# A two-layer graph network on one core: VectorE's copies, the second norm and the convolution steps moved to other units of a round, and the moments of y moved into the first layer

## The reference, cut to what matters

```
h = relu(layernorm(x));  x = x + L0(h, adj)       # 8 Euler steps of a linear flow on the graph
h = relu(layernorm(x));  x = x + L1(h, adj)

L1: L_norm = 2 L / lam_max(L) - I                 # L is adj itself here; one matrix for all batches
    x1 = relu(layernorm((L_norm x) Wc + bc) g1 + be1) + x
    q, k, v = x1 Wq, x1 Wk, x1 Wv                 # 4 heads of 32
    o = softmax(where(adj > 0, q k^T / sqrt(32), -1e9)) v
    x2 = layernorm(x1 + o Wo + bo) g2 + be2
    out = layernorm(x2 + gelu(x2 W1 + b1) W2 + b2) g3 + be3
```

## Time and profile before

| | |
|---|---|
| median of three runs | 867.99 us |
| the profiled execution | 868.01 us |
| its span (first to last instruction) | 866.2 us |
| PE busy | 818.8 us (95%) |
| DVE busy | 646.5 us (75%) |
| ACT busy | 530.5 us (61%) |
| POOL busy | 310.4 us (36%) |
| mean granted clock | 0.988 |

### The profile page before, as it was taken

One profiled execution on the slowest core, in us unless ns is written; L12 is line 12 of the kernel. 1 busy time (PEld: TensorE's weight loads), 2 busy tenths in 40 slices (PEclk: granted clock), 3 DMA queues, 4 the chain that ended last, 5 costly groups with the idle time before them and its releaser, 6 DMA issues.

```text
span 866.2 us, 18914 instructions
## 1 busy us (share of the span) xinstructions
PE 818.8 (95%) x6609; PEld 690.4 (80%) x6609; DVE 646.5 (75%) x2146; ACT 530.5 (61%) x1223; POOL 310.4 (36%) x406
## 2 busy tenths in 40 slices
PE   6999999999999999998999999999999999999992
PEld 5778989898989888976777777777777777778982
DVE  5956464645477656536899999999999998987998
ACT  4434243434322422325988888898888888887884
POOL 2011121212122415300445545555554545432654
PEclk9999999999999999998999999999999999999997
DMA  6000010101010100312434455423344444322243
GB/s 133 1 13 13 13 37 13 37 14 37 13 37 13 37 25 26 101 46 76 119 94 108 133 136 135 134 94 96 96 124 135 135 136 133 103 49 63 82 139 97
DMA packets 57514, 65.59 MB, mean 76 GB/s; under 512 B 5574, under 2 KB 32844, under 8 KB 57420
## 3 DMA queue, kind: packets, MB, share of 16 engines
q1 hardware_dynamic: 57120, 64.25, 26.6%
q10 hardware_dynamic: 300, 0.13, 0.1%
HBM read 39.59 MB, written 24.77 MB: 74 GB/s over the span
## 4 chain that ended last, share of the span: by engine, by line
PE 21%; DVE 12%; issue 8%; POOL 8%; ACT 3%; DMA 1%; DVEq 0%; SPq 0%; POOLq 0%
PE bank L1896 6%; PE bank L1954 4%; PE bank L1916 4%; PE bank L1882 3%; DVE prob L2062 2%; PE bank L381 2%; POOL z_norm L353 2%; POOL z_gain L349 2%; POOL x_bo L1834 2%; DVE stats L1666 2%; ACT prob L2004 2%; POOL rstd_b L230 2%; PE bank L385 1%; DVE prob L1661 1%; DVE z L2101 1%
## 5 line engine op out<-in xcount | busy, mean ns | idle before, releaser
L2004 ACT ACTIVATE prob<-prob,low 128x512 f32<-128x512 f32 x256 | 183.7, 718 | 28.2 <-DVE low L2062 25.8
L2062 DVE CUSTOM_DVE_ANT_0 prob<-bank,mask 128x512 f32<-128x512 f32 x256 | 171.0, 682 | 8.5 <-PE bank L1882 6.3
L1896 PE MATMUL bank<-ident,prob 128*128 128x128 f32 x1024 | 158.3, 277 | 1.4 <-ACT probT L1987 1.0
L1896 PEld LDWEIGHTS bank<-ident,prob 128*128 128x128 f32 x1024 | 120.8, 141 | 42.1 <-issue 30.6
L1882 PE MATMUL bank<-k_stack,q_stack 96*128 96x512 f32 x256 | 124.1, 485 | 8.6 <-DVE low L2062 7.3
L1987 ACT ACTIVATE probT<-bank 128x512 f32<-128x512 f32 x176 | 103.1, 586 | 22.9 <-PE bank L1896 21.4
L880 PE MATMUL bank<-B_hi,halves 128*128 128x384 f32 x384 | 106.7, 341 | 3.0 <-DVE C L1276 1.6
L851 PE MATMUL bank<-halves,P3T_hi 128*128 128x256 f32 x512 | 93.9, 285 | 0.9 <-DVE halves L1292 0.5
L851 PEld LDWEIGHTS bank<-halves,P3T_hi 128*128 128x128 f32 x512 | 80.5, 191 | 4.4 <-DVE halves L1292 1.3
L880 PEld LDWEIGHTS bank<-B_hi,halves 128*128 128x128 f32 x384 | 70.6, 189 | 6.4 <-DVE halves L1263 2.7
L851 PE MATMUL bank<-halves,P3T_lo 128*128 128x256 f32 x256 | 72.4, 283 | 0.0
(11 more groups left out here) (277 smaller groups left out, 1919.4 us busy)
## 6 DMA issues: line engine op xcount, KB each, us to landing
k_stack<-bounce_q SPq DMA_DIRECT2D x48, 256.0 KB, 4.0
q_stack<-bounce_k SPq DMA_DIRECT2D x48, 256.0 KB, 5.5
bounce_q<-k_parts SPq DMA_DIRECT2D x32, 256.0 KB, 2.2
bounce_k<-q_parts SPq DMA_DIRECT2D x32, 256.0 KB, 3.8
x_in<-in_x_dram SPq DMA_DIRECT2D x16, 256.0 KB, 2.8
spread<-inverse_sums SPq DMA_DIRECT2D x64, 64.0 KB, 2.1
out_dram<-probT SPq DMA_DIRECT2D x16, 256.0 KB, 2.4
y_shifted<-y_staging SPq DMA_DIRECT2D x14, 256.0 KB, 2.1
```

The costliest lines, as they stand in the source:

```text
L1896: last = pe.transpose(psum[2 + u % 2][:, mt * P:(mt + 1) * P], prob[u % RING][:, mt * P:(mt + 1) * P], ident[:, :])
L2004: act.activation(prob[u % RING][:, :], prob[u % RING][:, :], ACT.Exp, bias=low[:, u % TURNED:u % TURNED + 1], scale=-1.0, accum_out=row_su ...
L2062: dve.tensor_tensor_reduce(prob[u % RING][:, :], psum[u % 2][:, :], mask[:, u // HEADS, :], 1.0, 3e38, ALU.add, ALU.min, low[:, u % TURNED ...
```

## The change

- `MOMENTS_AT` puts the moments of y of batches 0 to 12 (VectorE) and their `h_scales` (GpSimd) into layer 0: two batches each in pairs 2, 3, 4 and 6, one in pair 7, and batches 9 to 12 behind the last pair's second step. Batches 13 to 15 stay in rounds 11 to 13 at unit 9. The scales of all batches now have tiles of their own.
- `DVE_COPIES` is (0, 4, 7, 12, 13) and no longer (0, 7, 11, 13, 15): VectorE copies at units 3, 7, 10, 15 and 0, and ScalarE copies the tiles 11 and 15 (at units 14 and 2) but no longer 4 and 12.
- The four convolution steps of TensorE stand at units 6, 7, 8 and 8.
- z2 stands at unit 13, behind the moments of z and a further mask.
- The second norm's moments stand at unit 6 and its z_std at unit 9; in round 18 they stay at 3 and 5.

```diff
+MOMENTS_AT = {2: (0, 1), 3: (2, 3), 4: (4, 5), LAM_PAIR: (6, 7), KEY_PAIR: (8,), PAIRS: (9, 10, 11, 12)}
...
                     if p < PAIRS - 1:
                         scales(2 * p + 3, 1)
+                    for done in MOMENTS_AT.get(p, ()):
+                        h_scales(pool, one, done)
...
-                h_scales(pool, one, 2, 0)
+                for b in MOMENTS_AT[PAIRS]:
+                    h_scales(pool, one, b)
...
-                    if step == (-1, "y0"):
-                        y_moments(dve, one, 0)
-                    if step == (-1, "y1"):
-                        y_moments(dve, one, 1)
...
                         T_lo(2, a)
                     early(p, "T_lo2")
+                    for done in MOMENTS_AT.get(p, ()):
+                        y_moments(dve, one, done)
                     early(p, "q")
...
-AT_CONV, AT_CONV_OUT, AT_Z, AT_Z_OUT, AT_Z_MOMENTS, AT_Z_STD = 6, 9, 10, 11, 12, 14
+AT_CONVS, AT_CONV_OUT, AT_Z, AT_Z_OUT, AT_Z_MOMENTS, AT_Z_STD = (6, 7, 8, 8), 9, 10, 11, 12, 14
 AT_Y_MOMENTS, AT_H = 9, (11, 12, 13)
-AT_RINV, AT_SPREAD, AT_SPREAD_OUT, AT_O, AT_PROJ, AT_Z2 = 0, 1, 1, 8, 11, 12
-AT_Z2_MOMENTS, AT_Z2_STD = 3, 5
+AT_RINV, AT_SPREAD, AT_SPREAD_OUT, AT_O, AT_PROJ, AT_Z2 = 0, 1, 1, 8, 11, 13
+AT_Z2_MOMENTS, AT_Z2_STD, AT_LAST_Z2 = 6, 9, (3, 5)
 TURN_LAG = 3
 VALUES_LAG = 9
 VALUES_STEP = 4
-DVE_COPIES = (0, 7, 11, 13, 15)
+DVE_COPIES = (0, 4, 7, 12, 13)
...
-                    if within(r, 0, BATCH - 3):
-                        h_scales(pool, one, r + 2, s)
+                    if within(r, MOMENTS_AT[PAIRS][-1] - 1, BATCH - 3):
+                        h_scales(pool, one, r + 2)
...
-                        if u == AT_Y_MOMENTS and within(r, 0, BATCH - 3):
+                        if u == AT_Y_MOMENTS and within(r, MOMENTS_AT[PAIRS][-1] - 1, BATCH - 3):
                             y_moments(dve, one, r + 2)
```

More of the change, by code:

```diff
@@ L159, in two_layers @@
         one.stats = tensor(whole, "stats_a", [P, NT, 6])
-        one.mv = tensor(whole, "mv_a", [P, NT, 2])
+        one.mv = tensor(whole, "mv_a", [P, BATCH, NT, 2])
         one.var_eps = tensor(whole, "ve_a", [P, NT])
-        one.rstd = [tensor(whole, f"rstd_a{i}", [P, NT]) for i in range(2)]
+        rstd_a, shift_a = (tensor(whole, n, [P, BATCH, NT]) for n in ("rstd_a", "shift_a"))
+        one.rstd, one.shift = ([tile[:, b, :] for b in range(BATCH)] for tile in (rstd_a, shift_a))
         one.minus_one = tensor(whole, "minus_one", [P, NT])
         one.mean_rstd = tensor(whole, "mean_rstd_a", [P, NT])
-        one.shift = [tensor(whole, f"shift_a{i}", [P, NT]) for i in range(2)]
         one.h = [tensor(whole, f"h{i}", [P, NT, D]) for i in range(2)]
@@ L230, in inverse_root, with h_scales @@
     pool.tensor_tensor(out=rstd[:, :], in0=var_eps[:, :], in1=exponent[:, :], op=ALU.pow).then_inc(pool_step, 1)
-def h_scales(pool, one, b, s):
-    inverse_root(pool, b, one.mv, one.mv_ready, one.var_eps, one.rstd[s], one.pool_step, one.h_ready, NT * (b - 1),
+def h_scales(pool, one, b):
+    inverse_root(pool, b, one.mv[:, b, :, :], one.mv_ready, one.var_eps, one.rstd[b], one.pool_step, one.scales, 2 * b,
                  one.exponent, one.pool_waited)
     pool.wait_ge(one.pool_step, 2 * b + 2)
-    pool.tensor_tensor(out=one.mean_rstd[:, :], in0=one.mv[:, :, 0], in1=one.rstd[s][:, :],
+    pool.tensor_tensor(out=one.mean_rstd[:, :], in0=one.mv[:, b, :, 0], in1=one.rstd[b],
                        op=ALU.mult).then_inc(one.scales, 1)
     pool.wait_ge(one.scales, 2 * b + 1)
-    pool.tensor_tensor(out=one.shift[s][:, :], in0=one.mean_rstd[:, :], in1=one.minus_one[:, :],
+    pool.tensor_tensor(out=one.shift[b], in0=one.mean_rstd[:, :], in1=one.minus_one[:, :],
                        op=ALU.mult).then_inc(one.scales, 1)
@@ L315, in y_moments @@
 def y_moments(dve, one, b):
-    moments(dve, b, lambda t: one.y[:, bass.ds(b * N + t * D, D)], one.stats, one.stats_ready, one.mv, one.mv_ready,
-            one.scales, 2 * b, one.dve_waited)
+    moments(dve, b, lambda t: one.y[:, bass.ds(b * N + t * D, D)], one.stats, one.stats_ready,
+            one.mv[:, b, :, :], one.mv_ready, one.scales, 0, one.dve_waited)
 def z_moments(dve, one, b):
@@ L684, in pair @@
                     x_and_bias(2 * p, 0)
-                    if p == LAM_PAIR - 1:
-                        for b in range(2):
-                            h_scales(pool, one, b, b)
                     if p < LAM_PAIR:
@@ L1761, in layer1 @@
         rstd3 = [row_sums[0][:, i * NT:(i + 1) * NT] for i in range(RING)]
-        shift3 = [*one.rstd, *one.shift]
+        shift3 = one.shift[0:RING]
         y_be3_ready, stats3_ready, mv3_ready, pool3, scales3, z3_std_ready, z3_gain_ready, result_ready = (
@@ L1946, in round_ @@
                             q_product(pe, one, A_BANK, r)
-                        if AT_CONV <= u < AT_CONV + NT and within(r, 2, BATCH - 2):
-                            if u == AT_CONV:
+                        if u in AT_CONVS and within(r, 2, BATCH - 2):
+                            if u == AT_CONVS[0]:
                                 pe.wait_ge(q_lo_ready, r + 1)
@@ L1951, in round_ @@
                                 pe.wait_ge(L_split, 2)
[L1952 to L1957, removed]
+                            for k in (k for k in range(NT) if AT_CONVS[k] == u):
+                                for n, (h_part, L_part) in enumerate(products(h_parts, L_parts)):
+                                    last = pe.matmul(A_BANK[:, :], h_part[:, k, :], L_part[:, k, :],
+                                                     start=k == 0 and n == 0, stop=k == NT - 1 and n == 2)
+                                if k == NT - 1:
+                                    last.then_inc(one.conv_psum, 1)
                         if u == AT_PROJ and leaves:
@@ L2104, in round_ @@
                             z_moments(dve, one, r + 1)
-                        if u == AT_Z2_MOMENTS and finishes:
+                        if u == (AT_Z2_MOMENTS if r < BATCH + 2 else AT_LAST_Z2[0]) and finishes:
                             f = r - 3
@@ L2111, in round_ @@
                             z_standard(dve, one, r + 1)
-                        if u == AT_Z2_STD and finishes:
+                        if u == (AT_Z2_STD if r < BATCH + 2 else AT_LAST_Z2[1]) and finishes:
                             dve.wait_ge(c_pool, 2 * f + 2)
```

7 lines of the change are left out of this document (1 added, 6 removed).

## The result

The changed kernel took 909.62 us (median of 4 runs, 907.84 to 910.93), the kernel before beside it 867.71: a ratio of 1.0479, 95% interval 1.0463 to 1.0496. The forecast was 909. It is the fastest of the four runs: its mean granted clock is 0.985, that of the others 0.979 to 0.983.

The account below looks back on a forecast made before the run. TensorE sets the pace, with 0.2 us of slack where GpSimd's chain and VectorE meet at z_std. 38.4 - 1.2 + 2.6 - 0.5 + 1.7 = +41.0 on 868.0 gives 909 us; range 889 to 936.

Parts of the forecast that it names:

- z2 makes z_std wait: Rounds 2 to 14: z2 behind the moments and a mask starts 1.95 us later; z_std idles 2.55 us for rstd_b.
- The copy of tile 12 and the copy on ScalarE: Tile 12's copy between two masks makes the spread 2.56 us late; tile 15's copy on ScalarE makes x1T +2.97.
- rival (2): Only z2's delay counts, ScalarE catching up or VectorE's copies filling the hole: 25.4 + 2.6 = 28.0, 896 us; chance 10%.
- Nothing is won back from K on, nor by lighter rounds of VectorE: TensorE shows no wait from K to unit 12; VectorE's 1.33 us less work in rounds 1 to 10 gains 0.
- 13 x 2.95 = 38.4: Rounds 2 to 14 of layer 1: period grows from 24.75 to 27.7 us, together +38.4 us.
- The clock: TensorE's 2.3 us wait per round might make it begin at half clock; the time would then be rival (1)'s.
- rival (1): The wait costs the clock too: spread to K's end at 1.2 GHz, 13 x 2.1 = 27 us more, 936; chance 20%.
- Layer 0 and the barrier: Pair 5 loses TensorE's 1.25 us wait, -1.2; at layer 0's end GpSimd's four `h_scales` let the barrier go later, +2.6.
- Rounds 15 and 16, -0.5: Round 16: TensorE's 1.23 us wait lies behind the second norm's moments, now moved to unit 6; -0.5 (0 to -1.5).
- Round 17, +1.7: Moments of batch 14 now come behind q_parts, so the last norm's first sum starts at 798.3, not 796.56: +1.7 us.
- The second norm at 0: Its 2.35 us on VectorE come later in the same free stretch of the round, with 2 us to spare: 0.
- Rival (3): x_bo's late start is harmless, z_std finds rstd_b ready, TensorE's three waits go: 853 to 861 us; chance 5%.

## Why the prediction was right, point by point

- **z2 makes z_std wait.** Right, and shown from both ends (z2 put back, x_bo moved out of the way) and alone in the kernel before. The idle time was forecast at 2.55 and is 2.19, the delay at 1.95 and is 1.67. The difference is in the handing over: before, z_std started 0.18 us after rstd_b's end, because VectorE's copy ended then, and the root started 1.71 after x_bo; now these are 0.03 and 1.58.
- **The copy of tile 12 and the copy on ScalarE.** Forecast +0.61 and +0.41 behind the delay of z_std; measured +0.60 and +0.42. Shown by the run with the old copies (0.98 per round). With it rival (2), z2's delay alone, falls.
- **Nothing is won back from K on, nor by lighter rounds of VectorE.** Right (14.25 for 14.29; the run with the moments alone). The convolution steps were not run alone; in the changed kernel's regular round TensorE has no wait between K and the scores of 559.07, so nothing in their place made it wait.
- **13 x 2.95 = 38.4.** Mis-sized: the regular round grew from a mean of 24.83 to 27.33, 13 x 2.50 = 32.5. Of the 0.45 too much, 0.28 is the handing over, and 0.15 that the round I walked is a short one of the kernel before (24.68; three of 13 are 25.2).
- **The clock.** The forecast was made without it; rival (1) gave it 2.1 us in every round. It fell in two rounds of 13, which are 1.65 and 1.18 longer; the moments of y in them account for little of that (0.09 in round 13). Where it fell in the experiments it cost 1.05 a round, half of what the rival took. So the rival's mechanism was seen in the experiments, but in the changed kernel none of the ten rounds with the one wait of 1.98 lost the clock. Two errors of 3 to 6 us met: 32.5 + 2.9 = 35.4 for 38.4. That the sum came within 1 us of the median (909 for 909.62) is luck.
- **Layer 0 and the barrier.** Forecast -1.2 + 2.6 = +1.4, measured +1.35, but by luck in part: in the profile of before the clock fell once between 50 and 60 us of layer 0, in that of the changed kernel it did not. In the run with the moments alone, where it fell too, K of batch 1 is +2.64: TensorE's wait at the border grew by 3.2 for the forecast 2.6 (four `h_scales`, 2.18 each where I had 1.98), and layer 0 gave back 0.6 for 1.2 (the wait of 1.25 in pair 5 is 0.34, not gone). Round 1 was 0.98 longer, with a granted clock of 0.90 on average in place of 0.92; I had that as a possible end of the range only.
- **Rounds 15 and 16, -0.5.** Wrong: q_parts stands at 45.17 us behind K of batch 15, before at 45.00.
- **Round 17, +1.7.** Right: +1.84.
- **The second norm at 0.** Right for this kernel, for another reason than I gave: alone it costs 9 us, and the change pays that only where moments of y are left in the rounds.
- **Rival (3), faster with x_bo out of the way.** Its condition could be made (z_std without a wait, TensorE's three waits gone), and its gain is 1.7 us at best, not the 7 to 15 it gave: another wait came in their place.
- **Slips in the working.** The walk gives K 2.97 later, the sum takes 2.95 (0.3 us in all). The lower end of the range comes to 891 by the lower ends beside the terms, not 889. The "second case below" of the paragraph on the clock is rival (1).

## What to carry to other kernels

When an instruction is moved on one engine, look up who waits for it on an engine that takes its work in order, and what stands behind that waiter: here an addition that nobody needed for two rounds held up a root that was needed at once. A slack of 2 us per round on an engine says nothing where the chain through two other engines has 0.2. And a wait that is taken out of one engine's way must be put where its own work collides with nobody; that wants a look at the durations, not only at the waits.

## What the runs showed of the hardware

**VectorE and GpSimd in each other's way.** The residual reads two tensors (z_norm and h). Beside x_bo it took 1.46 to 1.78 us in place of 0.69. In the kernel before both it and GpSimd's h_hi are let go by z_norm and start within 0.01 us of each other in the rounds 3 to 14, and one of the two takes 1.15 or 1.16 (timelines of VectorE and of GpSimd, rounds 5 and 6):

```profile
497.34 0.69 DVE L362 SCALAR_TENSOR_TENSOR x<-z_norm,h 128x512 f32<-128x512 f32 x1 [0.21 <-POOL z_norm L353]
...
522.09 1.15 DVE L362 SCALAR_TENSOR_TENSOR x<-z_norm,h 128x512 f32<-128x512 f32 x1 [0.22 <-POOL z_norm L353]
```

```profile
497.34 1.16 POOL L1824 CAST h_hi<-h 128x512 fp32r<-128x512 f32 x1
...
522.09 0.61 POOL L1824 CAST h_hi<-h 128x512 fp32r<-128x512 f32 x1
```

Where the residual loses, K is late: of the 13 rounds of the kernel before exactly the three with a residual of 1.15 are 25.1 to 25.2 us long, and the others, with 0.69, 24.7 to 24.8. The Trainium skill, *SBUF — State Buffer*, section "SBUF: two separate sides", says that a VectorE instruction with two SBUF inputs and a GpSimd instruction that reads SBUF take turns for one pair of ports, whole instructions at a time, whoever comes first; the traces agree (0.69 and 1.16, or 1.15 and 0.61).

**The clock within rounds.** In two kernels in which TensorE waits about 2 us in one place of a round (z2 moved alone, 1.96, and the old copies, 1.99) the granted clock fell in ten and 11 of 13 rounds, for part of the round to 0.50 (1.2 GHz), to 0.94 on average over the round. In the changed kernel, whose wait is as long (1.98 at 559.07), it fell in none of the ten rounds with that wait, and in two of the three where the wait stands in pieces. In the two runs that took the wait away (z2 back at unit 12, x_bo behind the norm) it fell in none of the 13. The Trainium skill, *TensorE: Matmul & The Clock Gate*, section "HAM oscillation — how this bites in real kernels", tells of loops that wait in each iteration and start the next at the half clock; the two experiments agree in most rounds, the changed kernel's regular rounds do not. What decides between them stays open.
